# A window scan with layer norms and an MLP: last 64 state channels in one packed pass, layer norms applied by ScalarE, and a new order of work on VectorE

## The reference, cut to what matters

```
w = _ln(w, ln1_w, ln1_b)                # w: 1024 windows, 49 tokens, 192 channels
xB = w @ Bm
h = xB[t] + h @ A                       # for each token t in turn, all windows at once
xr = h @ Cm
y = _ln(xr, ln2_w, ln2_b)
y = gelu(y @ W1 + b1) @ W2 + b2
x1 = x + xr + y
```

## Time and profile before

| | |
|---|---|
| median of 3 runs | 5249.16 us (5247.32 to 5250.15) |
| the profiled execution | 5251.68 us, its span 5249.8 us |
| busy share of the span | PE 87%, PEld 74%, DVE 78%, ACT 45%, POOL 50% |
| mean granted TensorE clock | 0.969 of full speed |
| from one slot of the scan to the next | 22.8 us |

### The profile page before, as it was taken

The page is one execution under the profiler, slowest core; times in us unless marked ns, Lnnn a source line. Parts: engine busy times, 40 slices in busy tenths (PEclk is TensorE's granted clock), DMA queues, the critical chain, the costliest instruction groups (busy, mean ns, idle before and its releaser), DMA issues.

```text
span 5249.8 us, 122985 instructions
## 1 busy us (share of the span) xinstructions
PE 4578.6 (87%) x42440; PEld 3889.0 (74%) x42440; DVE 4090.6 (78%) x7841; ACT 2355.9 (45%) x4594; POOL 2642.0 (50%) x1714
## 2 busy tenths in 40 slices
PE   0699999999999999996788888888888888888887
PEld 0588888888888888886667777677776776767676
DVE  6788888888888888884677777777777777777776
ACT  0244444444444444442444444445444444444444
POOL 0245554555454545453455555555555555555554
PEclk9999999999999999997899999999999999999999
DMA  7011111111111111111222222222222222222222
GB/s 310 26 38 39 39 41 37 39 39 41 37 39 39 41 38 39 39 41 43 55 63 67 67 65 65 66 68 64 68 65 66 68 64 68 65 66 66 67 64 55
DMA packets 407188, 310.70 MB, mean 59 GB/s; under 512 B 148203, under 2 KB 405435, under 8 KB 405947
## 3 DMA queue, kind: packets, MB, share of 16 engines
q1 hardware_dynamic: 404404, 307.93, 20.8%
q10 hardware_dynamic: 2736, 2.14, 0.1%
HBM read 145.48 MB, written 87.33 MB: 44 GB/s over the span
## 4 chain that ended last, share of the span: by engine, by line
PE 26%; SPq 15%; DMA 5%; issue 4%; ACT 2%; DVE 1%; POOL 0%; ACTq 0%; DVEq 0%; POOLq 0%
SPq L843 15%; PE ps_w L1190 8%; PE ps_s L1208 4%; DMA Kp<-K 4%; PE ps_w L1159 4%; PE ps_t L1216 4%; PE ps_v L1251 3%; PE ps_w L1147 2%; ACT K L947 1%; ACT E L960 0%; ACT oT L988 0%; DMA mask<-in_shift_mask 0%; PE ps_s L1127 0%; PE ps_s L1128 0%; POOL E L885 0%
## 5 line engine op out<-in xcount | busy, mean ns | idle before, releaser
L885 POOL TENSOR_TENSOR E<-E,ri 128x588 f32<-128x588 f32 x512 | 803.2, 1569 | 1260.8 <-DVE ri L1092 1260.8
L1190 PE MATMUL ps_w<-wp,oT 128*98 128x192 f32 x2048 | 434.0, 360 | 370.3 <-DMA Kp<-K 355.6
L969 ACT ACTIVATE PT<-ps_t 98x588 f32<-98x588 f32 x512 | 339.4, 663 | 863.0 <-PE ps_t L1216 863.0
L604 PE MATMUL ps_o<-w,g_hi 128*128 128x384 f32 x2352 | 710.3, 365 | 5.9 <-DVE g_lo L544 4.1
L1190 PEld LDWEIGHTS ps_w<-wp,oT 128*98 128x98 f32 x2048 | 355.0, 184 | 391.8 <-issue 202.4
L416 ACT ACTIVATE gF<-ps_g,b1f 128x512 f32<-128x512 f32 x588 | 406.1, 691 | 392.6 <-PE ps_g L635 389.9
L1082 DVE SCALAR_TENSOR_TENSOR L<-ps_s,bias 128x588 f32<-128x588 f32 x512 | 394.6, 771 | 186.6 <-PE ps_s L1208 178.5
L1071 DVE TENSOR_TENSOR yo<-ps_w,rs 98x384 f32<-98x384 f32 x256 | 141.3, 552 | 508.9 <-PE ps_w L1190 508.8
L604 PE MATMUL ps_o<-w,g_lo 128*128 128x192 f32 x2352 | 534.6, 254 | 0.0
L1216 PE MATMUL ps_t<-ident,E 128*98 128x128 f32 x3072 | 461.5, 289 | 76.5 <-POOL E L885 76.5
L1216 PEld LDWEIGHTS ps_t<-ident,E 128*98 128x98 f32 x3072 | 327.4, 132 | 240.8 <-POOL E L885 185.6
(11 more groups left out here) (203 smaller groups left out, 12402.4 us busy)
## 6 DMA issues: line engine op xcount, KB each, us to landing
xs<-in_x SPq DMA_DIRECT2D x8, 4704.0 KB, 22.3
xt<-in_x SPq DMA_DIRECT2D x98, 384.0 KB, 3.4
x_cells<-x SPq DMA_DIRECT2D x784, 48.0 KB
xb<-x_cells SPq DMA_DIRECT2D x128, 294.0 KB
Kp<-K SPq DMA_DIRECT2D x1536, 24.5 KB, 1.9
Vx<-V SPq DMA_DIRECT2D x512, 73.5 KB
out<-yo SPq DMA_DIRECT2D x128, 294.0 KB
gnr<-gn_rows SPq DMA_DIRECT2D x128, 192.0 KB
```

Source lines behind the costliest of these rows:

```text
L604: last = pe.matmul(dst, g[:, f, P * k:P * (k + 1)], w, start=(f == 0 and i == 0), stop=(f == FT - 1 and i == 1))
L885: pool.tensor_tensor(e, e, ri[p][:, :].unsqueeze(2).to_broadcast([P, HEADS, T]), ALU.mult)\
L1190: last = pe.matmul(ps_w(OUT1 if half else OUT0)[0:T2, C * a:C * (a + 1)], oT[d][p][:, k, :], wp[:, k, :], start=(k == 0), stop=(k == 1))
```

## The change

Three things change, all for the scan.

1. `Split` of A and B gets 64 more columns in its upper tiles, which hold the lower parts of the last 64 output channels (`beside`). One matmul then has the upper weights of these channels in its first 64 columns and their lower weights in the other 64, and the sums stand in partitions 0 to 63 and 64 to 127 of `ps_h[:, 1, :]`. The second half of the state sums has six matmuls instead of ten. The two halves of the sum are added outside TensorE.
2. Both layer norms are applied by ScalarE (four activations with scale and bias each) instead of VectorE. For that VectorE also takes the negated mean, and GpSimd multiplies it by the power.
3. VectorE's order is another: statistics of xn right behind the group norm, then lower parts of y, then those of h, then the second half of x1.

```diff
+            def packed_terms(self, data_hi, data_lo):
+                both = slice(self.cols - self.beside, self.cols + self.beside)
+                a_hi, _, b_hi, _ = self.parts
+                return ((a_hi[:, both], data_hi[:, 0, :]), (a_hi[:, both], data_lo[:, :]), (b_hi[:, both], data_hi[:, 1, :]))
...
+                            if parts.beside:
+                                pool.tensor_tensor(parts.lower_beside(t), full[:, t, P:C], parts.upper(t)[:, P:C],
+                                                   ALU.subtract)
...
@ ScalarE, slot
-                        for k, rows in enumerate((P, CB)):
-                            last = act.activation(h_hi[d][0:rows, k, :], ps_h[0:rows, k, :], ACT.Identity,
-                                                  bias=hbias[0:rows, k:k + 1])
-                        last.then_inc(s_hh, 1)
+                        act.activation(h_low[0:CB, :], ps_h[CB:P, 1, :], ACT.Copy).then_inc(s_hc, 1)
+                        act.activation(h_hi[d][:, 0, :], ps_h[:, 0, :], ACT.Identity, bias=hbias[:, 0:1])
                     if there(n):
                         act.wait_ge(s_t2, n + 1)
                         upper_parts(y_hi, ps_g).then_inc(s_yh, 1)
+                    if there(n + 2):
+                        act.wait_ge(s_of1, n + 3)
+                        for k in range(TPC):
+                            last = act.activation(xn[c][:, k, :], xn[c][:, k, :], ACT.Identity,
+                                                  bias=ofa[:, k:k + 1], scale=rsa[:, k:k + 1])
+                        last.then_inc(s_xn, 1)
+                    if there(n + 1):
+                        act.wait_ge(s_hb, n + 2)
+                        act.activation(h_hi[d][0:CB, 1, :], h_b[0:CB, :], ACT.Copy).then_inc(s_hh, 1)
...
+                    if there(n + 1):
+                        act.wait_ge(s_of2, n + 2)
+                        act.wait_ge(s_rsum, n + 2)
+                        upto(act, s_t2, n + 1)
+                        for k in range(TPC):
+                            last = act.activation(yb[:, k, :], tok_tile(ps_r, k), ACT.Identity,
+                                                  bias=ofb[:, k:k + 1], scale=rsb[:, k:k + 1])
+                        last.then_inc(s_y, 1)
@ GpSimd, slot, ahead of the residual (L443)
+                        pool.wait_ge(s_ve1, n + 3)
+                        pool.tensor_tensor(rsa[:, :], vea[:, :], neg_half[:, :], ALU.pow).then_inc(s_rs1, 1)
+                        pool.wait_ge(s_rs1, n + 3)
+                        pool.tensor_tensor(ofa[:, :], nma[:, :], rsa[:, :], ALU.mult).then_inc(s_of1, 1)
...
@ VectorE, slot, behind the group norm and the statistics (L519, L524)
+                        dve.tensor_scalar(nma[:, :], mva[:, :, 0], -1.0, None, ALU.mult)
...
+                        dve.wait_ge(s_hc, n + 2)
+                        dve.scalar_tensor_tensor(out=h_b[0:CB, :], in0=ps_h[0:CB, 1, :], scalar=hbias[0:CB, 1:2],
+                                                 in1=h_low[0:CB, :], op0=ALU.add, op1=ALU.add).then_inc(s_hb, 1)
+                        dve.wait_ge(s_hh, n + 2)
+                        dve.scalar_tensor_tensor(out=h_lo[d][:, :], in0=ps_h[:, 0, :], scalar=hbias[:, 0:1],
+                                                 in1=h_hi[d][:, 0, :], op0=ALU.add, op1=ALU.subtract)
+                        dve.tensor_tensor(h_hi[d][CB:P, 1, :], h_b[0:CB, :], h_hi[d][0:CB, 1, :],
+                                          ALU.subtract).then_inc(s_hl, 1)
...
-                            last = dve.tensor_scalar(xn[c][:, k, :], xn[c][:, k, :], mva[:, k, 0:1], rsa[:, k:k + 1],
-                                                     ALU.subtract, ALU.mult)
...
-                            last = dve.tensor_scalar(yb[:, k, :], tok_tile(ps_r, k), mvb[:, k, 0:1], rsb[:, k:k + 1],
-                                                     ALU.subtract, ALU.mult)
@ TensorE, slot
-                        for m, rows in enumerate((P, CB)):
-                            cols = slice(P * m, P * m + rows)
-                            terms = (*W_B.terms(xn_hi[d], xn_lo[d], cols), *W_A.terms(h_hi[d], h_lo[d], cols))
+                        first = slice(0, P)
+                        for m, terms in enumerate(((*W_B.terms(xn_hi[d], xn_lo[d], first),
+                                                    *W_A.terms(h_hi[d], h_lo[d], first)),
+                                                   (*W_B.packed_terms(xn_hi[d], xn_lo[d]),
+                                                    *W_A.packed_terms(h_hi[d], h_lo[d])))):
```

More of the change, by code:

```diff
@@ L105, in build @@
             M1 = sb("M1", [P, NT, C])
-            W_B, W_A, W_C = (Split(ctx, name, C) for name in ("wB", "wA", "wC"))
+            W_B, W_A = (Split(ctx, name, C, CB) for name in ("wB", "wA"))
+            W_C = Split(ctx, "wC", C)
             W_1 = Split(ctx, "w1", HID)
@@ L162, in _ @@
                         for t in range(2):
-                            act.activation(parts.parts[2 * t][:, :], full[:, t, :], ACT.Copy)
+                            act.activation(parts.upper(t), full[:, t, :], ACT.Copy)
                     act.activation(w2[:, :, 0, :], raw_2[:, :, :], ACT.Copy).then_inc(s_wh, 1)
@@ L175, in _ @@
                         for t in range(2):
-                            pool.tensor_tensor(parts.parts[2 * t + 1][:, :], full[:, t, :],
-                                               parts.parts[2 * t][:, :], ALU.subtract)
+                            pool.tensor_tensor(parts.lower(t), full[:, t, :], parts.upper(t), ALU.subtract)
+                            if parts.beside:
+                                pool.tensor_tensor(parts.lower_beside(t), full[:, t, P:C], parts.upper(t)[:, P:C],
+                                                   ALU.subtract)
                     pool.tensor_tensor(w2[:, :, 1, :], raw_2[:, :, :], w2[:, :, 0, :], ALU.subtract)
@@ L281, in build @@
             h_lo = [sb(f"h_lo{b}", [P, NTOK], f32r) for b in range(2)]
+            h_low, h_b = sb("h_low", [P, NTOK]), sb("h_b", [P, NTOK])
             yb = sb("yb", [P, TPC, C])
@@ L474, in _, with lower_parts @@
             def _(dve):
-                def lower_parts(hi, lo, full, bias=None):
+                def lower_parts(hi, lo, full):
                     for k, rows, dst in ((0, P, lo[:, :]), (1, CB, hi[CB:P, 1, :])):
[L478 to L483, removed]
+                        last = dve.tensor_tensor(dst, full[0:rows, k, :], hi[0:rows, k, :], ALU.subtract)
                     return last
@@ L526, in slot @@
                         dve.wait_ge(s_ag1, n + 3)
+                        dve.tensor_scalar(nma[:, :], mva[:, :, 0], -1.0, None, ALU.mult)
                         dve.tensor_scalar(vea[:, :], mva[:, :, 1], LN_EPS, None, ALU.add).then_inc(s_ve1, 1)
+                    if there(n):
+                        dve.wait_ge(s_yh, n + 1)
+                        lower_parts(y_hi, y_lo, ps_g).then_inc(s_yl, 1)
+                    if there(n + 1):
+                        d = 1 - c
+                        dve.wait_ge(s_hc, n + 2)
[6 more added lines that the diff above has]
+                                          ALU.subtract).then_inc(s_hl, 1)
+                    if there(n - 1):
+                        dve.wait_ge(s_w2, n)
+                        x1_half(1 - c, 1, s_xb, n).then_inc(s_x1, 1)
                     if there(n):
@@ L565, in slot @@
                         dve.tensor_tensor(two(res[d]), tok(ps_r), two(res[d]), ALU.add).then_inc(s_rsum, 1)
-                        dve.wait_ge(s_rs2, n + 2)
-                        upto(dve, s_t2, n + 1)
-                        for k in range(TPC):
-                            last = dve.tensor_scalar(yb[:, k, :], tok_tile(ps_r, k), mvb[:, k, 0:1], rsb[:, k:k + 1],
-                                                     ALU.subtract, ALU.mult)
-                        last.then_inc(s_y, 1)
                     if there(n):
@@ L614, in slot @@
                         upto(pe, s_hl, n)
-                        for m, rows in enumerate((P, CB)):
-                            cols = slice(P * m, P * m + rows)
-                            terms = (*W_B.terms(xn_hi[d], xn_lo[d], cols), *W_A.terms(h_hi[d], h_lo[d], cols))
+                        first = slice(0, P)
[3 more added lines that the diff above has]
+                                                    *W_A.packed_terms(h_hi[d], h_lo[d])))):
                             for k, (w, v) in enumerate(terms):
-                                last = pe.matmul(ps_h[0:rows, m, :], w, v, start=(k == 0), stop=(k == len(terms) - 1))
+                                last = pe.matmul(ps_h[:, m, :], w, v, start=(k == 0), stop=(k == len(terms) - 1))
                         last.then_inc(s_scan, 1)
```

39 lines of the change are left out of this document (18 added, 21 removed).

## The result

The changed kernel takes 5619.72 us (median of 4 executions, 5611.17 to 5623.43); the kernel before, run beside it, 5248.24 us (4 executions, 5237.88 to 5250.15). The ratio is 1.071, with a 95% interval of 1.0691 to 1.0729: 7.1% slower, where 5600 us was forecast. The profiled execution took 5611.17 us, its span is 5609.4 us, and the mean granted clock over it 0.939 (0.969 before). Of the runs further down, two executions of the kernel before with split stores (6943.82 and 7069.22 us) and one of the packing alone (5812.47 us) ran at a mean granted clock of 0.60, 0.59 and 0.74, and no ratio counts them. In the loop a slot takes 26.72 us on the mean from one group norm to the next, 22.82 us before; 91 × 3.90 = 355 of the 359.6 us by which the span is longer.

The account below looks back on a forecast made before the run. The prediction took the round x1, stores, load, group norm, x1 as the bound, not TensorE: 5251.7 + 91 x 3.9 (355) - 5 = 5602 us for the profiled execution, stated as 5600 us, 6.7% slower, range 5515 to 5705 us.

Parts of the forecast that it names:

- The round with the stores: Scan loop: x1, 14 stores, load, group norm, x1 sets the pace, growing from 22.8 to 26.7 us per slot.
- VectorE's part of the round: From group norm start to the end of x1 on VectorE: grows from a mean of 6.5 to 10.4 us.
- the four activations: ScalarE applying the layer norm to xn, ahead of the copy of h_b: 1.85 us together, overlap included.
- the multiplication on 4 columns: GpSimd multiplying the negated mean by the power: 0.19 us, bounded from above by the power's 1.01 us.
- VectorE's wait for the copy: VectorE, done with h_b, waits ahead of h_lo for ScalarE's copy: about 1.6 us per slot.
- the line through two sizes: Price of GpSimd's small multiplication, from 0.59 us at 192 columns and 1.81 us at 768: 0.19 us.
- the bias's 90 ns: ScalarE's added cost for a bias from a tile, taken again for the scale: 0.53 us per activation.
- rival C: Scan: TensorE's clock falls and TensorE becomes late; a 3.1 us fall loses 1.6 us, which is covered. Chance 8%.
- C's other case: TensorE's clock stays low over 10 us per slot, making TensorE the bound; with 14 us, 28.6 us per slot, 5780 us.
- The term outside the loop: Some six slots outside the loop, where shorter state sums win about 0.9 us each: 5 us less.
- the lower bound: Range's low end: four activations at 1.13 us, negated mean free; VectorE's part 9.5 us, round 25.8 us, 5520 us.
- rival A: Scan: TensorE sets the pace and the change is faster, 98 x 1.2 = 115 us less, 5134 us. Chance 4%.

Follow-up runs that it names:

- kernel before with split stores: The kernel before with the load of x issued between the two halves of the 14 stores: 5245.14 us, ratio 0.9998.
- packed kernel set free: The kernel before plus packed state sums, load of x between the store halves, and GpSimd's third sum put off behind the next group norm: 5143.62 us, ratio 0.9802.
- packed kernel: The kernel before with the packed state sums alone, its layer norms and its order otherwise kept: 5248.06 us, ratio 1.001.
- changed kernel with split stores: The changed kernel with the load of x issued between the two halves of the stores: 5415.60 us, ratio 1.0328 against the kernel before.

## Why the prediction was right, point by point

- **The round with the stores sets the pace, and TensorE does not.** Shown: its load releases the group norm in every slot of the changed kernel, two edits shorten the slot as foretold (25.52 us for 25.6 with the copy first, 24.16 us for 24.2 without the packing); x1 ahead of h shortens it by what VectorE's part lost (to 23.99 us), though that part was to be 6.4 us and was 7.75; and the load ahead of half the stores (24.57 us) ends the wait. Outside VectorE the two slots took 16.21 and 16.49 us, 16.3 were taken.
- **VectorE's part of the round.** 10.34 us measured, 10.4 predicted. The terms: the four activations 1.86 us (1.85 taken from the bias's price; a scale from a tile costs about the same), the multiplication on 4 columns 0.20 us (0.19), VectorE's wait for the copy 1.77 us (1.6), GpSimd's power 1.02 us. The two rows taken from elsewhere for want of better ones, the line through two sizes for the multiplication and the bias's 90 ns for the scale, were both right.
- **What it is made of.** Without the packing VectorE's part is 24.16 - 16.3 = 7.9 us, 1.4 us over the 6.5 of before: the statistics came in, and the holding up of the group norm went. The packing adds h_b's 0.74 us and the wait of 1.77 us, together 2.51 of the 2.56 measured. That wait is there because the copy of h_b stands on ScalarE behind xn, and xn behind GpSimd. The 1.4 us are read from the timeline (1.81 us from L544 to the lower parts of y come in, 0.5 us of holding up go); no run has the new order without ScalarE's layer norms, so the two were not separated.
- **TensorE.** Its 16 matmuls of the state sums take 3.67 us (1216.62 to 1220.29), 0.229 us each, and its need of 21.6 us was measured as a slot of 21.59 us in the packed kernel set free. It waits 3.0 us per slot for y, 3 to 4 were said. Its busy share is 88%, not 81%: the sum left out that its clock falls behind most of these waits. TensorE's timeline:

```profile
1224.40 0.36 PE L638 MATMUL ps_o<-w,g_hi 128*128 128x384 f32 x1
1226.75 0.71 PE L671 MATMUL ps_g<-y_hi,w_a_hi 128*128 128x512 f32 x1 [1.99 <-DVE y_hi L520]
1227.26 0.63 PE L671 MATMUL ps_g<-y_lo,w_a_hi 128*128 128x512 f32 x1
...
1230.50 0.40 PE L671 MATMUL ps_g<-y_hi,w_b_lo 128*128 128x512 f32 x1
1230.73 0.40 PE L671 MATMUL ps_g<-y_hi,w_a_hi 128*128 128x512 f32 x1
```

  Eight matmuls of 0.43 us instead of 0.23 lose 1.6 us; the window above gives a granted clock of 0.52 there, that is 1.2 GHz, and 1.00 behind it. This slot is one of the milder ones. In the slot before it TensorE waited 3.61 us, and the low clock lasted twice as long:

```profile
1199.55:1206.38 6.83, 6.19 (x15) 4.83 (x16) 4.16 (x7) 4.28 (x8) 1.52 (x3) 0.50 0.00 0
```

  From 400 to 2200 us a slot has 4.0 us at 1.2 GHz on the mean, which lose 2.0 us: 21.6 us of its own need, 2.0 us lost and 3.0 us of waiting make 26.6 us, and (21.6 + 2.0) / 26.7 is the measured 88%. In slots of 26.72 us this was covered, as rival C's sum had it for a short fall (1.6 us, a little less than came); C's other case, a clock that stays low for over 10 us, did not come.
- **GpSimd and L538.** Its last sum ended at 1246.73, 1.6 us ahead of L538 at 1248.35; in the slot before it was 0.3 us (1221.20 against 1221.52). L538 took 0.96 us in every slot of the stretch, so it was held up nowhere, as said, but with little to spare. GELU, which was given up to 1.1 us of delay, followed the copy without a gap at 1229.20, and in this slot the first block was no sooner complete (1228.54 + 0.63 = 1229.17), as its matmuls ran at half clock.
- **The sum.** 355 us in the loop against 355 predicted. The term outside the loop was wrong: 5 us were to go, and 4.6 us came. The loop's first group norm starts at 284.50 us (284.45 before), so the six slots ahead of it won nothing, and 3.9 of the 4.6 us lie in the attention, again at a lower clock (0.94 here, 0.95 in the row of the kernel before further up):

```profile
2787.20:5609.40 2822.20, 2325.47 (x29260) 1948.34 (x29260) 2001.43 (x3351) 1331.55 (x2819) 1501.16 (x912) 0.94 0.24 65
```

  So the profiled execution is 9 us over its forecast of 5602 us. It was the fastest of four, and the median is 20 us over 5600 us (0.4%).
- **Slips in its sums.** With its own terms the lower bound is 9.6 us on VectorE and about 5530 us, not 9.5 and 5520, and rival A's 98 x 1.2 is 118 us, not 115. Neither changes the forecast.

The prediction took the kernel before to be bound by one round. That was enough for the changed kernel, where this round is 2.1 us above the next one (26.72 against 24.57 us with the load ahead of half the stores), and too simple for the kernel before: with the stores' round taken away GpSimd's sums stood in the way at a slot of 22.80 us, with these gone too the path from the state sums over ScalarE at 22.78, and with y first VectorE's nearly unbroken row of work at 22.78. The last of the three is read from waits alone; no edit removed it. TensorE's 22.53 us were never reached without the packing; what it would take to reach them was not tried. That one more instruction costs VectorE only 0.3 us in the packed kernel shows in the starts, which follow each other by 0.61 to 0.70 us there and by 0.71 to 0.77 us in the kernel before; why they do is open.

## What to carry to other kernels

When an engine is busy for 100% and still waits a little in every slot, look for a round that crosses a queue and ends at the same time; here it held no matmul, so less work for TensorE bought almost nothing and each microsecond between the load and x1 cost a full one. An optimisation can be right and its place wrong: the same packing won 2%, changed nothing, or cost 4.5%, depending on the rounds around it and on what stood ahead of its last copy. Compare the stages of two traces one by one, too: a total can stay the same while one stage wins 20 us and another loses them. Before work is moved away from an engine, write down for each piece whether it stood inside or outside the round, and look for all chains of about that length: here taking them away one or two at a time gave nothing.

## What the runs showed of the hardware

- An instruction of VectorE with two inputs in SBUF and one of GpSimd do not run beside each other: L542 and L544 of the changed kernel with split stores took 2.07 and 2.48 us instead of 0.96, GpSimd's sum between them 2.55 instead of 1.86, each in turn. The changed kernel has it too: L577 took 1.74 us beside GpSimd's residual and 0.69 us in its next turn. The Trainium skill, "SBUF — State Buffer", section "SBUF: two separate sides", says that such a VectorE operation and a GpSimd operation take a shared pair of ports as an exclusive lock for the whole instruction; these times agree.
- An activation of 192 columns with scale and bias from tiles takes 536 ns from SBUF and 510 ns from PSUM. The groups of the stretch, busy us and mean ns of one behind the bar:

```profile
L432 ACT ACTIVATE xn<-xn,ofa,rsa 128x192 f32<-128x192 f32 x271 | 126.2, 536 | 338.3 <-POOL ofa L480 338.3
L461 ACT ACTIVATE yb<-ps_r,ofb,rsb 128x192 f32<-128x192 f32 x268 | 115.1, 510 | 196.9 <-POOL ofb L499 196.9
```

- In the changed kernel TensorE waits 1.9 to 3.7 us ahead of the first layer in each of the 67 slots from 400 to 2200 us. In that stretch its clock was granted at half 60 times, 41 times for 3.4 us and 19 times for 6.8 us; the fall came within 2 us of the end of such a wait, and at a few of the waits it did not come. In the change without its packing, where these waits are 1.0 to 1.7 us, it fell once in the same stretch.
- The same 29260 TensorE instructions of the attention kept TensorE busy for 2319 us in the kernel before and for 2341 us in the packing alone, at a granted clock of 0.95 and 0.94.
